# A sequential recurrence of 256 steps: the second square root reads the first root and a sum formed from its argument; six VectorE sums a step; table rows laid out by GpSimd

## The reference, cut to what matters

```python
def step(M, kv):
    k_t, v_t = kv
    v_pred = jnp.einsum('bf,bfd->bd', k_t, M)
    surprise = jnp.linalg.norm(v_t - v_pred, axis=-1, keepdims=True)
    delta = k_t[:, :, None] * v_t[:, None, :]
    M = M + eta_c[None, :, None] * surprise[:, :, None] * delta
    return (_ln2(M), None)          # (M - mean) * rsqrt(var + 1e-5), mean and var over f, d
```

## Time and profile before

| | us |
|---|---|
| median of three runs | 2175.63 |
| the three runs | 2175.63, 2182.12, 2169.21 |
| the profiled execution, its own time | 2169.05 |
| its span, first to last instruction | 2167.2 |
| granted TensorE clock, mean of the span | 0.878 |

### The profile page before, as it was taken

One profiled execution on the slowest core, in us unless ns is written; L12 is line 12 of the kernel. 1 busy time (PEld: TensorE's weight loads), 2 busy tenths in 40 slices (PEclk: granted clock), 3 DMA queues, 4 the chain that ended last, 5 costly groups with the idle time before them and its releaser, 6 DMA issues.

```text
span 2167.2 us, 36000 instructions
## 1 busy us (share of the span) xinstructions
PE 1850.6 (85%) x12384; PEld 1219.6 (56%) x12384; DVE 1315.7 (61%) x4959; ACT 976.3 (45%) x2490; POOL 318.3 (15%) x455
## 2 busy tenths in 40 slices
PE   6888677888887999999998888997899864999888
PEld 5455455655665577875556667543544541963333
DVE  3687899999898445774333667251311432469886
ACT  2422566666665232334443223553453213537666
POOL 0000000000000002310000002004044034307642
PEclk9999799999897677999999558997999967989989
DMA  3001200000000000000001100021023102625662
GB/s 116 1 13 27 44 20 26 26 20 26 26 20 12 31 1 2 3 2 0 1 1 78 42 0 1 1 88 36 6 20 59 78 20 58 92 65 97 101 105 42
DMA packets 93284, 76.13 MB, mean 35 GB/s; under 512 B 22320, under 2 KB 85168, under 8 KB 92336
## 3 DMA queue, kind: packets, MB, share of 16 engines
q1 hardware_dynamic: 85424, 65.31, 13.1%
q0 software_dynamic: 7680, 8.53, 2.2%
HBM read 48.86 MB, written 23.51 MB: 33 GB/s over the span
## 4 chain that ended last, share of the span: by engine, by line
PE 56%; DVE 20%; ACT 10%; issue 4%; DMA 3%; SPq 2%; another core or an unknown queue 2%; POOL 2%; PEld 0%; DVEq 0%; PEldq 0%; ACTq 0%; POOLq 0%
PE ps L204 52%; ACT sm L213 6%; DVE big L217 3%; DVE sm L225 3%; PE ps L208 2%; DMA d_pt<-big 2%; PE ps L2503 2%; ACT big L213 2%; DVE big L231 1%; ACT big L212 1%; DVE tmp L221 1%; SPq L2590 1%; SPq L877 1%; DVE sm L221 1%
## 5 line engine op out<-in xcount | busy, mean ns | idle before, releaser
L213 ACT ACTIVATE tmp<-ps,bi 128x512 f32<-128x512 f32 (+1 forms) x226 | 153.7, 683 | 196.3 <-PE ps L204 178.7
L213 ACT ACTIVATE sm<-sm 128x1 f32<-128x1 f32 x513 | 174.6, 340 | 141.3 <-DVE sm L225 88.5
L204 PE MATMUL ps<-big,mw 128*128 128x512 f32 (+3 forms) x476 | 217.1, 554 | 10.1 <-DVEq L252 5.6
L204 PE MATMUL ps<-big,co 128*128 128x256 f32 (+1 forms) x360 | 151.1, 540 | 65.3 <-ACT big L213 44.6
L213 ACT ACTIVATE big<-ps 128x512 f32<-128x512 f32 (+1 forms) x296 | 151.0, 558 | 74.2 <-PE ps L204 71.7
L231 DVE TENSOR_REDUCE big<-ps 128x2 f32<-128x512 f32 x256 | 160.4, 673 | 16.4 <-PE ps L204 15.8
L204 PEld LDWEIGHTS ps<-ke,big 32*128 32x128 f32 (+2 forms) x1632 | 136.1, 196 | 52.3 <-ACT big L212 33.4
L204 PE MATMUL ps<-ke,big 32*128 32x128 f32 (+2 forms) x1632 | 150.5, 293 | 9.5 <-ACT big L212 1.8
L204 PE MATMUL ps<-ke 48*128 48x256 bf16 (+4 forms) x638 | 130.1, 319 | 31.3 <-DVE big L217 16.9
L217 POOL TENSOR_TENSOR big<-big,co 128x512 f32<-128x512 f32 x32 | 40.1, 1274 | 690.8 <-ACT big L212 690.8
L204 PE MATMUL ps<-tmp,mw 128*128 128x512 f32 x288 | 140.3, 599 | 0.7 <-ACT tmp L212 0.7
(11 more groups left out here) (256 smaller groups left out, 3769.8 us busy)
## 6 DMA issues: line engine op xcount, KB each, us to landing
mw<-d_tab SPq DMA_DIRECT2D x32, 328.0 KB, 3.5
mw<-m SPq DMA_DIRECT2D x2, 4096.0 KB, 12.7
d_pt<-big SPq DMA_DIRECT2D x32, 192.0 KB
ke<-d_pt SPq DMA_DIRECT2D x72, 64.0 KB
big<-d_pt SPq DMA_DIRECT2D x72, 64.0 KB
mw<-d_pt SPq DMA_DIRECT2D x48, 64.0 KB
d_xs<-big SPq DMA_DIRECT2D x1, 2560.0 KB, 16.6
big<-d_xs SPq DMA_DIRECT2D x5, 512.0 KB, 7.0
```

Of the source, the lines that this page charges most:

```text
L204: return e.matmul(out, lhsT, rhs, start=start, stop=stop)
L213: return e.activation(out, in_, f, bias=0.0 if bias is None else bias, scale=scale, **kw)
```

## The change

In a step, the second root is now taken of first root times a number of `D` plus `A_`, and `A_` is a sum made from `zv`, the first root's argument, and from `G_`, which is made before `zv` is ready to be read. So `X2` is gone, with `YE`, `CE`, `C2` and the instructions that fed them. A step has six VectorE sums, in this order: `Y` (written into the plane `SAME`/`NEXT` of the tile `DP`), the table sum of `D`, the pair `D[:, t+1, 9:11]` (called E in the prediction), `zv`, `G_`, `A_`. One semaphore `sc_both` counts the first root and `A_`. The head forms its tile in two parts, `exA` and `ex`, with two products into one bank; a diagonal of `exA` is written by ScalarE. The table's rows are laid out anew by GpSimd after each table has landed (`rows_pool`: a copy of 64 numbers, from chunk 1 on a product of one, a copy of 8, a memset of 8), and the head and the first step wait for it; GpSimd's two clearings come after the first of these. Signs of two table columns are turned in the stage before. Two masks are applied once ahead of the scan (`others_dve`), and `state_dve` sets more tiles.

```diff
-            cp(e, TAB[:, 8 * g:8 * g + 8, 0:78:11], Q5.rearrange("p c t s -> p c (t s)")[:, :, 0:64:9]).then_inc(dv, 1); dn.up()
+            ts(e, TAB[:, 8 * g:8 * g + 8, 0:78:11], Q5.rearrange("p c t s -> p c (t s)")[:, :, 0:64:9], -1.0, None, MU).then_inc(dv, 1); dn.up()
...
+        exA, ex = SC[:, 384:480], SC[:, 480:552]
+        exA3, ex3 = exA.rearrange("p (j x) -> p j x", x=12), ex.rearrange("p (j x) -> p j x", x=9)
+        WS = WT[:, 448:768]
+        DP = WS[:, 0:216]
+        D = DP[:, 0:96].rearrange("p (j x) -> p j x", x=12)
+        SAME = DP[:, 0:192].rearrange("p (k x) -> p k x", x=96)
+        NEXT = DP.rearrange("p (k x) -> p k x", x=108)
+        GM = [WS[:, 216 + 24 * i:240 + 24 * i].rearrange("p (j x) -> p j x", x=3) for i in range(3)]
+        M8 = WS[:, 288:312].rearrange("p (j x) -> p j x", x=3)
         vw, vwr, mk, mk2 = (TMP[:, 8, 128 * i:128 * i + 128] for i in range(4))
         EK4 = [BIG[2 + c // 16][:, 256 * (c % 16):256 * (c % 16) + 256].rearrange("p (k n) -> p k n", k=2) for c in range(NC)]
...
+                    e.wait_ge(*sc_exa(c))
+                    e.wait_ge(*sc_dg(c))
+                    mm(e, PS[:, 7, 0:96], K("blk"), exA, start=True, stop=False)
                     e.wait_ge(*sc_ex(c))
-                    mm(e, PS[:, 7, 0:96], K("blk"), ex).then_inc(sc_exp.sem, 1)
...
+                        if a == 2:
+                            e.wait_ge(*sc_dd(c))
+                            act(e, exA[:, 0:92:13], one8r, ACT.Identity, scale=x10[:, 9:10]).then_inc(sc_dg.sem, 1)
                 for t in range(C):
                     e.wait_ge(*sc_z(8 * c + t + 1))
-                    act(e, Wst[:, t:t + 1], zv, ACT.Sqrt, scale=-1.0, bias=YE[:, 1:2]).then_inc(sc_w.sem, 1)
-                    e.wait_ge(*sc_x(8 * c + t + 1))
-                    act(e, Pv, X2[:, 0:1], ACT.Sqrt, scale=Wst[:, t:t + 1], bias=CE[:, 0:1]).then_inc(sc_r.sem, 1)
+                    act(e, Wst[:, t:t + 1], zv, ACT.Sqrt, scale=-1.0, bias=D[:, t, 9:10] if t else None).then_inc(sc_both, 1)
+                    e.wait_ge(sc_both, 2 * (8 * c + t + 1))
+                    if c and t == 0:
+                        e.wait_ge(*sc_cp(c))
+                    act(e, Pv, Wst[:, t:t + 1], ACT.Sqrt, scale=D[:, t, t:t + 1], bias=A_[:, 0, 0:1]).then_inc(sc_r.sem, 1)
                     if c and t < 3:
                         scaled_act(e, 5 + t)
...
         def scan_pool(e):
+            rows_pool(e, 0)
             e.memset(BIG[2][:, :], 0.0).then_inc(sc_zero.sem, 1)
             e.memset(BIG[3][:, :], 0.0).then_inc(sc_zero.sem, 1)
+            for c in range(1, NC):
+                rows_pool(e, c)
+
+        def rows_pool(e, c):
+
+            i = free + 656 * (c % RTB)
+            e.wait_ge(s_rt[c % RTB], 16 * (c // RTB) + 16)
+            cp(e, MW[:, i:i + 664].rearrange("p (j x) -> p j x", x=83)[:, :, 0:71:10],
+               RT[c % RTB][:, :, 9:80:10]).then_inc(sc_tp.sem, 1)
+            if c:
+                tt(e, GM[c % 3][:, 0, 0:1], G3[:, 2, c, 0:1], one8_[:, 0:1], MU).then_inc(sc_tp.sem, 1)
+            e.wait_ge(*sc_tp(3 * c + 1))
+            cp(e, MW[:, i:i + 652:93], RT[c % RTB][:, :, 81]).then_inc(sc_tp.sem, 1)
+            e.wait_ge(*sc_tp(3 * c + 2))
+            e.memset(RT[c % RTB][:, :, 81], 1e-5).then_inc(sc_tab.sem, 1)
 
...
+        def others_dve(e, dn):
+
+            other = one8c.rearrange("p (c s) -> p c s", c=1).broadcast_to((128, NC, 8))
+            tt(e, G3[:, 0], G3[:, 0], other, MU).then_inc(dv, 1); dn.up()
+            tt(e, NBt, NBt, other, MU).then_inc(dv, 1); dn.up()
...
+            tt(e, vr, DP[:, 202:203], rr, MU).then_inc(dv, 1); n_v = dn.up()
             added_dve(e, c, 1, pT1, PS[:, 2, 256:384], sc_p0e)
-            tt(e, rr, rR, rR, MU).then_inc(dv, 1); n_rr = dn.up()
-            ts(e, one8r, one8_, rR, 2.0, MU, MU).then_inc(dv, 1); dn.up()
+            e.wait_ge(dv, n_v)
...
-            ttr(e, tmp8, pv, one8_, x10[:, 8:9]).then_inc(dv, 1); dn.up()
+            tt(e, ex3[:, :, 8], one8r, pv, MU).then_inc(dv, 1); dn.up()
             e.wait_ge(dv, n_L)
             stt(e, x10[:, 0:8], NBt[:, c, :], PS[:, 3, 257:258], x10[:, 0:8], MU, AD).then_inc(dv, 1); n_x = dn.up()
-            e.wait_ge(dv, n_s)
-            ts(e, ex3[:, :, 11], one8_, rr, None, MU).then_inc(dv, 1); n_f = dn.up()
-            e.wait_ge(dv, n_f)
-            tt(e, ex3[:, :, 0:10], *outer(one8r, 8, x10, 10), MU).then_inc(sc_ex.sem, 1)
-            e.wait_ge(dv, n_q)
-            ts(e, CE[:, 0:1], qv, 1e-5, None, AD).then_inc(dv, 1); n_c = dn.up()
+            e.wait_ge(dv, max(n_s, n_g))
+            e.wait_ge(*sc_tab(c + 1))
+            stt(e, exA3[:, :, 9:12], M8, rq, GM[c % 3], MU, AD).then_inc(sc_exa.sem, 1)
+            e.wait_ge(dv, n_x)
+            tt(e, ex3[:, :, 0:8], *outer(one8r, 8, x10[:, 0:8], 8), MU).then_inc(sc_ex.sem, 1)
...
+        def sums_at(plane, t):
+            return plane[:, :, 12 * t + 10:95:12]
+
+        def pair_of(ap, n):
+            return ap.rearrange("p (k j) -> p k j", k=1).broadcast_to((128, 2, n))
 
...
+                ts(e, zv, D0[:, 0, 8:9], D0[:, 0, 9:10], 0.0, SU, MN).then_inc(sc_z.sem, 1)
                 if c:
-                    cp(e, Dall, PS[:, 7, 0:96]).then_inc(dv, 1); e.wait_ge(dv, dn.up())
-                n_A = ahead_dve(e, dn, T_, 0)
-                n_E = start_dve(e, dn, T_, 0)
+                    cp(e, DP[:, 0:96], PS[:, 7, 0:96]).then_inc(sc_cp.sem, 1)
+                e.wait_ge(*sc_z(8 * c + 1))
+                stt(e, A_, pair_of(T_[:, :, 0], 8), zv, D0[:, :, 10:12].rearrange("p j k -> p k j"), MU, AD).then_inc(sc_both, 1)
                 if c == 0:
                     cross_dve(e, 1)
                 for t in range(C):
-                    w_ = Wst[:, t:t + 1]
+                    n, w_ = C - t, Wst[:, t:t + 1]
+                    e.wait_ge(sc_both, 2 * (8 * c + t + 1))
                     if t == C - 1:
-                        e.wait_ge(*sc_w(8 * c + t + 1))
                         ttr(e, tmp8, Wst, one8_, wown).then_inc(dv, 1); n_w = dn.up()
-                        e.wait_ge(dv, n_A)
-                        stt(e, X2[:, 0:1], C2[:, t, 0:1], w_, D[:, t, 9:10], MU, AD).then_inc(sc_x.sem, 1)
+                        stt(e, sums_at(NEXT, t), pair_of(D[:, t:8, t], n), w_, A_[:, :, 0:n], MU, AD).then_inc(sc_last.sem, 1)
                         weights_dve(e, dn, c + 1, n_w)
-                        e.wait_ge(*sc_x(8 * c + t + 1))
-                        stt(e, qv, X2[:, 0:1], w_, qv, MU, AD).then_inc(sc_last.sem, 1)
                         break
-                    e.wait_ge(*sc_w(8 * c + t + 1))
-                    e.wait_ge(dv, n_A)
-                    stt(e, twice(X2), twice(C2[:, t, 0:2]), w_, twice(D[:, t, 9:11]), MU, AD).then_inc(sc_x.sem, 1)
-                    stt(e, D[:, t + 1:8, t:10], T_[:, t + 1:8, 11 * t:10 * t + 10], w_, D[:, t + 1:8, t:10], MU, AD).then_inc(dv, 1); n_D = dn.up()
-                    e.wait_ge(*sc_x(8 * c + t + 1))
+                    if c and t == 0:
+                        e.wait_ge(*sc_cp(c))
+                    stt(e, sums_at(NEXT, t), pair_of(D[:, t:8, t], n), w_, A_[:, :, 0:n], MU, AD).then_inc(dv, 1); n_Y = dn.up()
+                    stt(e, D[:, t + 1:8, t + 1:9], T_[:, t + 1:8, 11 * t + 1:10 * t + 9], w_, D[:, t + 1:8, t + 1:9], MU, AD).then_inc(dv, 1); dn.up()
+                    e.wait_ge(dv, n_Y)
+                    stt(e, D[:, t + 1, 9:11], T_[:, t + 1, 80:82], D[:, t, 10:11], SAME[:, :, 12 * t + 22], MU, AD).then_inc(dv, 1); n_E = dn.up()
+                    e.wait_ge(*sc_r(8 * c + t + 1))
                     e.wait_ge(dv, n_E)
-                    stt(e, YE[:, 0:4], X2, w_, CE, MU, AD).then_inc(dv, 1); n_Y = dn.up()
-                    e.wait_ge(dv, n_D)
-                    stt(e, D[:, t + 1:8, 11], D[:, t + 1:8, t], w_, D[:, t + 1:8, 11], MU, AD).then_inc(dv, 1); n_F = dn.up()
-                    e.wait_ge(*sc_r(8 * c + t + 1))
-                    e.wait_ge(dv, n_Y)
-                    stt(e, zv, D[:, t + 1, 8:9], Pv, YE[:, 1:2], MU, MN).then_inc(sc_z.sem, 1)
-                    if t + 2 < C:
-                        n_A = ahead_dve(e, dn, T_, t + 1)
-                    stt(e, CE[:, 0:3:2], YE[:, 0:5:4], 1e-5, YE[:, 2:3].broadcast_to((128, 2)), MU, AD).then_inc(dv, 1); n_E = dn.up()
-                    if t + 2 < C:
-                        e.wait_ge(dv, n_E)
-                        n_E = start_dve(e, dn, T_, t + 1)
+                    stt(e, zv, D[:, t + 1, 8:9], Pv, D[:, t + 1, 9:10], MU, MN).then_inc(sc_z.sem, 1)
+                    stt(e, G_[:, :, 0:n - 1], pair_of(T_[:, t + 1:8, 11 * t + 11], n - 1), D[:, t + 1, 9:10], sums_at(SAME, t + 1), MU, SU).then_inc(dv, 1); n_G = dn.up()
+                    e.wait_ge(dv, n_G)
+                    e.wait_ge(*sc_z(8 * c + t + 2))
+                    stt(e, A_[:, :, 0:n - 1], pair_of(T_[:, t + 1:8, 11 * t + 11], n - 1), zv, G_[:, :, 0:n - 1], MU, SU).then_inc(sc_both, 1)
```

(24 more changed lines are left out.)

65 lines of the change are left out of this document (23 added, 42 removed).

## The result

The changed kernel took **2158.20 us** (median of 4 runs, 2150.75 to 2164.62), the kernel before 2178.53 on the same chip (4 runs): a ratio of 0.9916, 95% interval [0.9889, 0.9942]. A second comparison, with 11 and 19 runs, gave 2160.36 against 2169.58, a ratio of **0.9954 [0.9935, 0.9974]**. So the change is worth 0.5 to 0.8%, 10 to 18 us; the forecast was -8.1 us. 2158.20 lies in the predicted range (2151 to 2183), 9.3 us under the forecast (2167.5) and 2 us outside its own range (2160 to 2174). The first comparison is a gain of more than 0.5%, which the prediction gave a chance of 0.39; the larger one, 0.46%, is on the side that it gave 0.51. The profiled execution took 2164.62 us, its span is 2162.3. Measured between the barriers at its two ends, the recurrence took 475.87 us; before it was 489.26.

What follows compares the result with a forecast made beforehand. The prediction took VectorE's chain of dependent sums to bound the recurrence's step after the change. Its terms, -12.6 us for the chunks and +4.45 for the start, made -8.1: 2167.5 us, own range 2160 to 2174, whole range 2151 to 2183.

Steps and rivals of the forecast that it cites:

- Six of seven steps gain nothing: Steps from t = 1: second root 0.19 us earlier, but VectorE's chain of sums sets the step, mean 1.265 us.
- 0.02 more for each of the chained sums: Step's upper bound: if broadcast and strided operands cost each of four chained VectorE sums 0.02 us more, 1.34 us.
- A late second wait costs 0.105: Ahead of the next first-root sum: its second wait, for VectorE's own pair, comes last and adds 0.105 us.
- Rival (1): In the steps, the second wait is cheap: step 1.20 us, -22.6 us in all, 2153 us; chance 0.20.
- The transition from t = 0: A chunk's first step: A reads PSUM directly, 1.235 us instead of 1.37, a gain of 0.13.
- The head: From a chunk's last first-root sum to the next chunk's first: merged instructions shorten it by 0.27 us to 5.29.
- Rival (2): In the head, the second product and longer scalings eat the 0.27 us gain: +8.1 us, 2175.6 us; chance 0.16.
- Per chunk: First transition -0.13, head -0.27, other steps -0.02: -0.42 us a chunk, -12.6 us over 30.
- The start: Stage opening: GpSimd lays out table 0's rows before clearing, so key copies and chunk 1's update come 4.45 us later.
- Rival (4): At the opening, the late start does not count because chunk 1 waits for something else: -12.6 us, 2163 us; chance 0.08.
- GpSimd's rows cost nothing: In the chunks: GpSimd's four row operations, 0.82 us at most, run beside other work and cost 0.
- rival (3): In the chunks, GpSimd's row operations hold VectorE's sums: +23.8 us, so +15.7 in all, 2191.3 us; chance 0.08.

Runs made afterwards that it cites:

- run 3: Changed kernel with the two waits ahead of zv swapped, the late one for VectorE's pair E written first: 2142.1 us, 0.9886 of the kernel before.
- run 9: Kernel before with its two waits ahead of zv swapped, the late one for the second root written last: 2184.4 us against 2164.66, 1.0100.
- Run 10: Changed kernel with each chunk's first sum made by two instructions again: 2159.4 us against 2164.66 for the kernel before, 0.9979.
- run 2: Changed kernel with GpSimd's first clearing put ahead of table 0's rows: 2159.66 us, 0.9942 of the kernel before.
- run 7: Changed kernel with 30 more GpSimd copies of 64 numbers after the table rows of each chunk from 1 on: 2151.35 us, one run.
- run 8: Changed kernel with 30 more GpSimd memsets of 64 numbers after the table rows of each chunk from 1 on: 2158.89 us, one run.
- run 5: Kernel before with five instead of two products that nobody reads in each chunk's head: 2166.81 us against 2164.95, 1.0005.
- run 6: Changed kernel without the two products that nobody reads in each chunk's head: 2156.74 us against 2164.95 for the kernel before, 0.9963.

## Why the prediction was right, point by point

- **Six of seven steps gain nothing: right, by the mechanism named.** The second root starts 0.67 after zv (292.87), predicted 0.66, and VectorE's chain sets the next step. Predicted 1.29 at t = 1 falling to 1.24 at t = 6, measured 1.326 to 1.238. The six steps together are 0.06 longer than before where -0.02 was said. The term that was too small is the length of the wide sums: at t = 1 A took 0.239 for the 0.225 assumed, Y 0.244 for 0.23, and D was issued 0.15 after Y, not 0.14, so E starts at 1.01 instead of 0.97. The bound "0.02 more for each of the chained sums" covered it. The prediction's own sign of being wrong, a step over 1.3, is met at t = 1 and 2 (1.326 and 1.302) and not by the mean of the six, 1.277.
- **A late second wait costs 0.105: right, and shown by runs 3 and 9.** The prediction said that an instruction with a second wait starts later when that second one comes last, and that VectorE waiting for itself is no different; both hold. It is a matter of the written place: 0.10 if the late wait is written last, 0.04 if first. What it did not do is ask what the other order would give: its own kernel before had the late wait first and a gap of 0.03. Rival (1), "the second wait is cheap", priced a step at 1.20; run 3 made exactly these steps, by one swapped line (mean of the six 1.21), and 14 us came with it.
- **The transition from t = 0**: predicted 1.235, measured 1.227 from root to root (before 1.425 by that measure and 1.37 from sum to sum, as the chunk's first sum took 0.16 then and takes 0.22 now) and 1.23 from sum to sum. The gain is the 0.13 predicted.
- **The head**: predicted 5.29 from the last zv to the first, measured 5.28 (298.54 to 303.82). Its parts: ahead of the reduction +0.04 (0.04 said), reduction to outer product 0.92 (0.91 said), from there -0.21 (-0.19 said). Run 10 shows that half of the merging alone is worth 0.20. Rival (2), the head gives nothing, is refuted.
- **Per chunk** -0.36 instead of -0.42: the difference is the steps' 0.08, less 0.02 that the first transition and the head gained beyond what was said.
- **The start**: +3.7 us instead of +4.45. The clearing starts 4.5 us after the opening, as predicted, and the update 4.6 later. The 0.9 between that and 3.7 lies behind the update, 0.7 of it in chunk 1's head (6.44 for 7.16). That VectorE's beginning was shorter (its one-number copy beside the clearing took 0.15, where an 8-number copy had taken 3.18) only lengthened TensorE's wait for the copies: with run 2's order chunk 1's first root starts as early (23.1 us after the barrier), and chunk 2 at 43.8, where it was 44.0. Rival (4) is refuted by run 2: the earlier clearing gave 3.4 us back.
- **GpSimd's rows cost nothing**: right; rival (3), the one with the loss, is refuted by runs 7 and 8.
- **Sum**: by terms -0.36 x 29 - 0.4 + 3.7 = -7.1 us, for -8.1 predicted. The measured gain is 10 us in the larger comparison (5.6 to 14.1 by its interval) and 18 in the smaller. What the prediction did not have is the clock's part: two long heads in the one profile of the kernel before, one shorter one in those of the changed kernel, 4.6 us in the profile, and the odd steps (1.7). The stage's own gain, 13.4, is 5.3 above the forecast of 8.1, and more than all of that is this part; that the total measured in the larger comparison, 10, lies nearer is the scatter of the other stages, and luck. To see it would have needed a look at the lengths of all chunks before: the two of 17.6 us stood in the trace.

**Open.** What makes a low stretch fall on a head. In the three profiles of the kernel before and its variants (runs 5 and 9) heads of 6.6 to 8.6 us stand in the middle of the stage, ten in all; in the nine of the changed kernel and its variants one (run 2) has two there, of 7.08 and 6.88, and the others have a long head only in chunks 0, 1 and 30. So the clock's part of the gain seems to belong to the change, but no run isolates what in it does this. Three more or two fewer of the unread products in a head don't decide it (runs 5 and 6); larger numbers were not tried. The odd steps, 0.1 to 0.5 longer, come in the same chunks and steps in the kernel before and in run 5 (1.77 at the first step of chunk 12 in both), and the changed kernel's six are the same in its two profiles and in runs 2, 6 and 8, so they belong to the program and not to chance. They stand elsewhere in runs 7 and 10, where VectorE has instructions more, and not in run 8, where only GpSimd has; their cause is open. TensorE also still waits for the key copies (6.82 in run 2); what of it could be gained no run shows.

## What to carry to other kernels

Where an instruction has two waits, write the one that comes last first: 0.07 us an instruction, which in a chain of 7 x 31 steps took 14 us off the stage, as much as the whole rewriting of the recurrence (13.4). When one operation is taken out of a ping-pong between two engines, add up the other engine's own chain of dependent instructions before counting the gain: here the root came 0.19 earlier and six of seven steps gained nothing. And a small job put ahead of a long one in a queue moves all that waits for the long one: ask which of the two is due first.
